# ALiBi attention: row maxima taken per half of the queries, and the order of the first group of heads

## The chip, the cores and the metric

The kernel runs on one core of a Trainium2 chip. The metric is the device time of one execution in microseconds (us). The core has TensorE (PE, matrix products and transposes), VectorE (DVE), ScalarE (ACT, exponentials among others), GpSimd (POOL), and SyncE (SP), which issues DMAs.

## What is computed

Two transformer layers on 1024 tokens of width 512, each an attention and a feed-forward part with a layer norm after each. The change touches the attention of the second layer: 32 heads of width 16, clipped and layer-normed queries and keys, ALiBi bias, causal softmax.

```python
qkv = jnp.clip(jnp.einsum('bsd,ed->bse', hidden_states, w_qkv), -CLIP_QKV, CLIP_QKV)
q, k, v = jnp.split(qkv, 3, axis=-1)
q = _layer_norm(q, q_ln_w, q_ln_b)
k = _layer_norm(k, k_ln_w, k_ln_b)
scores = jnp.einsum('bqhd,bkhd->bhqk', q, k) * scale
scores = jnp.where(causal[None, None], scores + slopes[:, None, None] * rel, -jnp.inf)
probs = jax.nn.softmax(scores, axis=-1)
attn = jnp.einsum('bhqk,bkhd->bqhd', probs, v).reshape(B, S, D)
```

## The kernel before

`program` runs five stages one after the other: `stage_latent` and `stage_mla` (first attention), `stage_front` (first feed-forward part and the projections of q and k of the second layer), `stage_alibi` (the second attention) and `stage_gated` (the rest). The change lies in `stage_alibi` and in two tables ahead of it.

`stage_alibi` works on eight groups of four heads (`GROUPS`, `HG`). For each group it needs queries and keys with the head dimension on the partitions. `build(chunk, which)` transposes queries (0) or keys (1) of two groups on PE (L1367), scales them on DVE (L1503), and ACT and DVE or POOL split them into a high and a low part. `move(eng, g, which, landed)` then copies the pieces of a group with twelve DMAs of 64 KB (L1322) into `qk_bufs`, of which there are three sets (`BUFS`): SP moves queries, POOL moves keys and loads the ALiBi rows. A set holds two blocks of rows of queries (`queries(b, s)`, one for each pair of heads) and four of keys.

The softmax needs the maximum of each score row ahead of the exponentials. `m(g, n)` is one of 24 units (`M_UNITS`): for a pair of heads `s`, the query tile `i` (128 queries, the last tile first) and the key half, PE computes the scores of both heads (L1392, with a mask matmul L1395 on the diagonal) into one of two PSUM slots `sm`, and DVE reduces them to negated maxima (L1515). After the last unit `top` joins the two key halves on DVE and splits the result into two parts (L1525 to L1530), `rows` transposes it on PE (L1401), DVE copies it to `mT` (L1535), and SP's `maxima(g)` writes it with four DMAs (L1334) into two extra rows of the query buffers. From then on a product of keys and queries already holds score minus maximum. `e(g, n)`, 48 a group, is such a product for a key tile, a half of the queries and a head (L1416, mask L1419), into one of three PSUM banks; ACT takes the exponential (L1475). `pv(g, c)` multiplies the four heads' probabilities of a chunk by the values (L1432). `out` copies the result (L1482), `back` transposes it back (L1440) and DVE divides by the row sums.

`alibi_order` writes out one list that PE, ACT and DVE each follow, every engine taking its own kinds. Within group g the 48 e and 12 pv are interleaved with the 24 m of group g+1 (the list `ahead`), its top, the first four m of group g+2, and the rows of group g+1, spread by the number of columns. For group 0 nothing runs ahead: its list begins with the two builds, the value projections `v` of four of the eight token tiles (`project_v`, twelve matmuls each, L78 called from it, into the three banks that e uses later), the 24 m with the other four v between the first ones, top, m(1,0), rows, and three more m of group 1.

SP has its own order: the moves of group 0's queries, a wait for all eight v (`vp`; the buffers that group 1 uses hold operands of v until then), the moves of group 1's queries, `maxima(0)`, and then for each group the moves of group g+2 and `maxima(g+1)`. POOL waits for the same `vp` before it clears and fills the buffers of groups 1 and 2 (`pads`, `load_rows`, `move_keys`), and then clips the values (`values`, L1587) that pv reads.

## Time and profile before

| | us |
|---|---|
| median of 3 runs (lowest to highest) | 1590.12 (1585.02 to 1590.92) |
| the profiled execution | 1588.67 |
| its span, first to last instruction | 1586.8 |
| PE busy | 1477.9 (93%) |
| DVE busy | 893.4 (56%) |
| ACT busy | 805.4 (51%) |
| POOL busy | 549.5 (35%) |
| mean granted clock of TensorE | 0.966 of 2.4 GHz |

The profile is of one execution. Its times are us from the first instruction; names such as L1392 are lines of the kernel. A timeline row gives start, duration, engine, line and operation, output and inputs, and in square brackets how long the engine sat idle before it and what ended that time. The stage that changes runs from about 935 to 1308 us. "e(0,0)" below is the score product at 998.12 us, the first on line L1416.

### The profile page before, as it was taken

To read this page: it belongs to the slowest core of one execution; us is meant where nothing else is said; L and a number is where in the kernel's file an instruction comes from. 1 tells how busy PE (TensorE), PEld (TensorE's weight loads), DVE (VectorE), ACT (ScalarE), POOL (GpSimd) and SP (SyncE) were. 2 spreads that over 40 slices of the span, in tenths; PEclk is the share of its full clock that TensorE was granted. 3 is DMA by queue.
4 is the path that set the end of the run, shared out by engine and by line. 5 is a ranking of instruction groups with operands and counts; after the bars stand their busy time and mean duration, and the time that the engine had idled before them with its cause. 6 is when DMAs were issued, how large, how long until landed. Compare 5 with 4: busy or idle time off the path is not lost. (4 is left out here: it accounts for less than half of the span.)

```text
span 1586.8 us, 23991 instructions
## 1 busy us (share of the span) xinstructions
PE 1477.9 (93%) x8320; PEld 1036.9 (65%) x8320; DVE 893.4 (56%) x1346; ACT 805.4 (51%) x1731; POOL 549.5 (35%) x506
## 2 busy tenths in 40 slices
PE   5499999999999999999968988899999989999996
PEld 4377676667767766776635866555555548888885
DVE  3145454555544555554565745666666616877877
ACT  2266555556655555666423430455555565433343
POOL 0444433344443334444015044223232004444442
PEclk9699999999999999999978997999999999999998
DMA  3135544544454354445530034333333205000000
GB/s 120 49 46 51 50 34 47 42 40 43 48 50 34 46 47 40 39 46 41 84 60 1 1 44 69 48 55 55 55 55 55 88 2 226 1 1 0 1 27 27
DMA packets 46289, 74.06 MB, mean 47 GB/s; under 512 B 18704, under 2 KB 24848, under 8 KB 45328
## 3 DMA queue, kind: packets, MB, share of 16 engines
q1 hardware_dynamic: 41872, 62.70, 28.4%
q0 software_dynamic: 4352, 10.49, 4.4%
q8 instruction: 41, 0.67, 0.2%
q14 instruction: 24, 0.20, 0.0%
HBM read 40.39 MB, written 2.10 MB: 27 GB/s over the span
## 5 line engine op out<-in xcount | busy, mean ns | idle before, releaser
L677 DVE TENSOR_REDUCE nmax<-sc 128x1 f32<-128x128 f32 (+7 forms) x256 | 192.4, 752 | 182.7 <-PE sc L465 182.7
L1515 DVE TENSOR_REDUCE pm<-l_sm 128x2 f32<-128x1024 f32 (+1 forms) x192 | 179.8, 957 | 112.6 <-PE l_sm L1395 61.8
L1475 ACT ACTIVATE l_probs<-l_banks 128x512 f32<-128x512 f32 (+3 forms) x384 | 171.2, 493 | 136.1 <-PE l_banks L1419 97.1
L608 ACT COPY pt<-tb 128x512 f32<-128x512 f32 (+3 forms) x256 | 129.2, 505 | 201.4 <-PE tb L479 199.8
L600 ACT ACTIVATE probs<-sc,nmax 128x128 f32<-128x128 f32 (+7 forms) x256 | 190.6, 745 | 56.2 <-DVE nmax L677 55.9
L479 PE MATMUL tb<-ident,probs 128*128 128x128 f32 x1152 | 174.1, 276 | 2.1 <-ACT pt L608 1.1
L78 PE MATMUL sc<-k_h,q_h 128*128 128x512 f32 (+3 forms) x384 | 144.7, 377 | 22.1 <-POOL q_l L748 14.6
L1416 PE MATMUL l_banks<-qk_bufs 128*128 128x512 f32 (+3 forms) x384 | 141.3, 412 | 5.2 <-ACT l_probs L1475 3.8
L1392 PE MATMUL l_sm<-qk_bufs 128*128 128x512 f32 (+3 forms) x384 | 130.8, 412 | 12.9 <-DVE pm L1515 6.5
L503 PE MATMUL mb<-pt,ckv 128*64 128x512 f32 (+3 forms) x768 | 137.8, 494 | 0.1
L78 PE MATMUL sc<-k_l,q_h 128*128 128x512 f32 (+3 forms) x384 | 133.7, 348 | 0.0
L78 PE MATMUL sc<-k_h,q_l 128*128 128x512 f32 (+3 forms) x384 | 133.6, 348 | 0.0
L479 PEld LDWEIGHTS tb<-ident,probs 128*128 128x128 f32 x1152 | 123.5, 142 | 8.1 <-DVE pt L685 4.0
L668 DVE TENSOR_TENSOR x_tok<-mb,x_tok 128x512 f32<-128x512 f32 x128 | 88.0, 688 | 61.0 <-PE mb L78 59.5
L1416 PEld LDWEIGHTS l_banks<-qk_bufs 128*128 128x128 f32 x384 | 72.1, 193 | 67.5 <-ACT l_probs L1475 42.7
L78 PEld LDWEIGHTS sc<-k_h,q_h 128*128 128x128 f32 x384 | 72.8, 190 | 58.1 <-issue 34.8
L730 POOL TENSOR_TENSOR ol_l<-ol_f,ol_h 128x512 fp32r<-128x512 f32 x32 | 41.3, 1292 | 192.0 <-ACT ol_h L587 191.9
L748 POOL TENSOR_TENSOR q_l<-late,q_h 128x1024 fp32r<-128x1024 f32 x32 | 76.0, 2375 | 51.4 <-ACT q_h L593 51.3
L503 PEld LDWEIGHTS mb<-pt,ckv 128*64 128x64 f32 x768 | 49.7, 136 | 65.5 <-issue 57.3
L1918 POOL TENSOR_TENSOR wall_l<-gated_late,wall_h 128x512 fp32r<-128x512 f32 x44 | 57.1, 1319 | 97.9 <-ACT wall_h L1824 97.9
L1977 DVE RECIPROCAL late<-late 128x512 f32<-128x512 f32 x27 | 90.5, 3352 | 0.8
L1392 PEld LDWEIGHTS l_sm<-qk_bufs 128*128 128x128 f32 x384 | 75.4, 208 | 23.7 <-DVE pm L1515 13.7
(263 smaller groups left out, 3145.2 us busy)
## 6 DMA issues: line engine op xcount, KB each, us to landing
gated_late<-in_gated SPq DMA_DIRECT2D x11, 768.0 KB, 14.0
wout<-in_w_out SPq DMA_DIRECT2D x16, 512.0 KB, 7.1
late<-late SPq DMA_DIRECT2D x128, 64.0 KB, 2.0
rb<-rT SPq DMA_DIRECT2D x64, 128.0 KB, 8.8
qk_bufs<-late SPq DMA_DIRECT2D x96, 64.0 KB, 5.0
qk_bufs<-late POOLq DMA_DIRECT2D x96, 64.0 KB, 5.9
nope_t<-in_nope_by_dim SPq DMA_DIRECT2D x16, 192.0 KB, 5.6
late<-in_gated SPq DMA_DIRECT2D x3, 768.0 KB, 9.1
```

Source lines behind the costliest of these rows:

```text
L78: last = pe.matmul(out, l, r, start=start and n == 0, stop=stop and n == len(terms) - 1)
L479: last = pe.transpose(tb[TB[g]][:, b, :], probs[n % 4][:, (j0 + b) * P:(j0 + b + 1) * P], keep.ident[:])
L503: last = pe.matmul(mb[g][64 * e:64 * e + 64, off:BANK], keep.ckv[:, j, :], pt[g][:, e, j, off:BANK], start=(j == 0), stop=(j == 4 * g + 3))
L600: act.activation(probs[s][:, 0:w], sc[n % 2][:, 0:w], ACT.Exp, bias=nmax[:, s:s + 1], accum_out=ssum[:, n:n + 1]).then_inc(exped, 1)
L608: act.copy(pt[i // 4][:, e, j0:j0 + nb, (i % 4) * P:(i % 4 + 1) * P], tb[TB[g]][:, 0:nb, :]).then_inc(pt_act, 1)
L668: dve.tensor_tensor(keep.x[:, j, :], mb[OUT_BANK[j]][:], keep.x[:, j, :], ALU.add).then_inc(mb_read[OUT_BANK[j]], 1)
L677: dve.tensor_reduce(nmax[:, n % 4:n % 4 + 1], sc[n % 2][:, 0:(n // 2 + 1) * P], AX.X, ALU.max, negate=True).then_inc(negmax, 1)
L1392: last = pe.matmul(dst[:, par, 0:w], queries(b, s)[:, i * P:(i + 1) * P], keys(b, 2 * s + par)[:, c0:c0 + w], start=True, stop=not diagonal)
L1416: last = pe.matmul(banks[:, at, 0:w], keys(b, h)[:, j * P:(j + 1) * P], queries(b, h // 2)[:, q0:q0 + w], start=True, stop=not diagonal)
L1475: act.activation(probs[(NC * g + c) % RING][:, h, 0:w], banks[:, (E_STEPS * g + n) % SLOTS, 0:w], ACT.Exp).then_inc(exped, 1)
L1515: dve.tensor_reduce(pm[g % 2][:, :, s, i, half], slot(("m", g, n))[:, :, 0:w], AX.X, ALU.max, negate=True).then_inc(freed, 1)
L1977: dve.reciprocal(den[:], den[:]).then_inc(rec_ok, 1)
```

## The change

The maxima are kept in two halves of the queries: part 0 for query tiles 0 to 3, part 1 for tiles 4 to 7. `M_UNITS` takes tiles 3, 2, 1, 0 first, then 7, 6, 5, 4. `top`, `rows` and `maxima` exist per part, each on half of the data, so a group has two of each, and `rows_in` has a semaphore per part; e(g, n) waits for part 0 at n = 0 and for part 1 at n = 16, from where its queries are of the second half. The query buffers are laid out so that a half of both pairs is contiguous, which makes each row of a query move two pieces. In the list, six of the eight v stand ahead of the first m, and a v is four items, one for each quarter of the contraction; the last two are placed, quarter by quarter, behind m(0,0) to m(0,7). Group 0's top and rows of part 0 follow, then four more m, then its e(0,0..15) and pv(0,0..2) between m(0,13..23), then part 1. POOL waits for `v_ev` instead of `vp` and clips the values of group 0 ahead of the pads of group 1, those of group 1 behind its key moves.

The diff, without the lines that only pass the new arguments on:

```diff
@@ -1194,14 +1194,17 @@
     k[:, :, 0] = k[:, :, 1] = 1.0
     q[:, :, 2], q[:, :, 3], q[:, :, 4], q[:, :, 5] = sh, sl, -pos, -pos
     k[:, :, 2], k[:, :, 3], k[:, :, 4], k[:, :, 5] = pos, pos, sh, sl
+    q = np.ascontiguousarray(q.reshape(GROUPS, 2, EX, 2, 2, BANK).transpose(0, 1, 2, 4, 3, 5)).reshape(q.shape)
     return q, k
 
 
 CHUNKS = [(j, half) for half in range(2) for j in range(4 * (half + 1))]
 NC = len(CHUNKS)
 E_STEPS = HG * NC
-M_UNITS = [(s, i, half) for i in reversed(range(ST)) for half in range(i // 4 + 1) for s in range(HG // 2)]
+M_UNITS = [(s, i, half) for i in (3, 2, 1, 0, 7, 6, 5, 4) for half in range(i // 4 + 1) for s in range(HG // 2)]
 NM = len(M_UNITS)
+M_HALF = 4 * (HG // 2)
+C_HALF = 4
 AHEAD = 4
 
 
@@ -1220,27 +1223,41 @@
 
 def alibi_order():
 
-    order = [("build", 0, 0), ("build", 0, 1)] + [("v", 0, j) for j in range(4)]
-    for n in range(NM):
-        order.append(("m", 0, n))
-        if n % 2 == 1 and n // 2 < 4:
-            order.append(("v", 0, 4 + n // 2))
-    order += [("top", 0, 0), ("m", 1, 0), ("rows", 0, 0)]
+    order = [("build", 0, 0), ("build", 0, 1)] + [("v", k, j) for j in range(6) for k in range(DK)]
+    late_v = [("v", k, j) for j in (6, 7) for k in range(DK)]
+    for n in range(M_HALF):
+        order += [("m", 0, n), late_v[n]]
+    order += [("top", 0, 0), ("m", 0, M_HALF), ("rows", 0, 0)]
+    order += [("m", 0, n) for n in range(M_HALF + 1, M_HALF + 5)]
+    rest = list(range(M_HALF + 5, NM))
+    at = 0
+    for c in range(C_HALF):
+        for h in range(HG):
+            order.append(("e", 0, HG * c + h))
+            while at < len(rest) and at * C_HALF * HG <= (HG * c + h) * len(rest):
+                order.append(("m", 0, rest[at]))
+                at += 1
+        if c >= 1:
+            order.append(("pv", 0, c - 1))
+    order += [("m", 0, n) for n in rest[at:]]
+    order += [("top", 0, 1), ("m", 1, 0), ("rows", 0, 1)]
     order += [("m", 1, n) for n in range(1, AHEAD)]
     for g in range(GROUPS):
-        ahead = [("m", g + 1, n) for n in range(AHEAD, NM)] if g + 1 < GROUPS else []
+        ahead = []
         if g + 1 < GROUPS:
-            ahead += [("top", g + 1, 0)]
+            ahead += [("m", g + 1, n) for n in range(AHEAD, M_HALF)] + [("top", g + 1, 0), ("m", g + 1, M_HALF), ("rows", g + 1, 0)]
+            ahead += [("m", g + 1, n) for n in range(M_HALF + 1, NM)] + [("top", g + 1, 1)]
         if g + 2 < GROUPS:
-            ahead += [("m", g + 2, 0), ("rows", g + 1, 0)] + [("m", g + 2, n) for n in range(1, AHEAD)]
+            ahead += [("m", g + 2, 0), ("rows", g + 1, 1)] + [("m", g + 2, n) for n in range(1, AHEAD)]
         elif g + 1 < GROUPS:
-            ahead += [("rows", g + 1, 0)]
+            ahead += [("rows", g + 1, 1)]
         if g % 2 == 0 and g // 2 + 1 < GROUPS // 2:
             ahead[2:2] = [("build", g // 2 + 1, 0)]
-            ahead[5:5] = [("build", g // 2 + 1, 1)]
-        done, total = 0, sum(chunk_cols(c)[1] * HG for c in range(NC))
+            ahead[6:6] = [("build", g // 2 + 1, 1)]
+        first = C_HALF if g == 0 else 0
+        done, total = 0, sum(chunk_cols(c)[1] * HG for c in range(first, NC))
         at = 0
-        for c in range(NC):
+        for c in range(first, NC):
             for h in range(HG):
                 order.append(("e", g, HG * c + h))
                 done += chunk_cols(c)[1]
...
         mT = al.sb("mT", [HG * 2 * ST, P], F32R)
         rsum = al.sb("rsum", [P, ST, HG])
         sm = [al.ps(f"l1_sm{i}", [P, 2, BANK]) for i in range(2)]
         banks = al.ps("l1_banks", [P, SLOTS, BANK])
         pv = al.ps("l1_pv", [P, BANK])
...
@@ -1305,7 +1324,12 @@
 
         def queries(b, s):
 
-            return keep.bufs[:, 6 * b + s, :]
+            pair = keep.bufs[:, 6 * b:6 * b + 2, :].rearrange("p a b -> p (a b)")
+            return pair.rearrange("p (half s c) -> p s half c", half=2, s=2)[:, s]
+
+        def query_cols(b, s, c0, w):
+
+            return queries(b, s)[:, c0 // BANK, c0 % BANK:c0 % BANK + w]
 
         def keys(b, h):
 
@@ -1319,26 +1343,28 @@
                 dst, parts = ((queries(b, h // 2), (0, 0, 1)), (keys(b, h), (2, 3, 2)))[which]
                 for n, w in enumerate(parts):
                     r0 = KR * (h % 2) + EX + HD1 * n
-                    eng.dma_start(dst[r0:r0 + HD1, :].bitcast(F32), stages[w][src, :]).then_inc(landed[b], 16)
+                    eng.dma_start(dst[r0:r0 + HD1].bitcast(F32),
+                                  stages[w][src, :] if which else stages[w][src, :].rearrange("p (half c) -> p half c", half=2)).then_inc(landed[b], 16)
 
         with nc.Block() as block:
 
             @block.sync
             def _(sp):
-                def maxima(g):
-                    sp.wait_ge(freed, uses["rows", g, 0] + 1)
+                def maxima(g, part):
+                    sp.wait_ge(freed, uses["rows", g, part] + 1)
                     for par in range(2):
                         for c in range(2):
-                            r, src = KR * par + c, (2 * par + c) * 2 * ST
+                            r, src = KR * par + c, MAXIMA * part + (2 * par + c) * ST
                             b = 6 * (g % BUFS)
-                            sp.dma_start(keep.bufs[r:r + 1, b:b + 2, :].bitcast(F32),
-                                         mT[src:src + 2 * ST, :].bitcast(F32)).then_inc(rows_in, 16)
+                            sp.dma_start(keep.bufs[r:r + 1, b + part, :].bitcast(F32),
+                                         mT[src:src + ST, :].bitcast(F32)).then_inc(rows_in[part], 16)
 
                 sp.wait_ge(low, 1)
                 move(sp, 0, 0, moved)
                 sp.wait_ge(vp, ST)
                 move(sp, 1, 0, moved)
-                maxima(0)
+                maxima(0, 0)
+                maxima(0, 1)
                 for g in range(GROUPS):
                     if g + 2 < GROUPS:
                         if g >= 1:
@@ -1351,7 +1377,8 @@
                             sp.wait_ge(alibi_in[done % BUFS], LOADS * (done // BUFS + 1))
                         prefetch_gated(sp, io, keep)
                     if g + 1 < GROUPS:
-                        maxima(g + 1)
+                        for part in range(2):
+                            maxima(g + 1, part)
 
             @block.tensor
             def _(pe):
...
@@ -1368,13 +1395,16 @@
                                             keep.ident[:])
                     last.then_inc(turned, 1)
 
-                def project_v(j):
-                    from_one(pe, v_ev, j - SLOTS + 1)
-                    rows, terms = slice(j * P, (j + 1) * P), []
-                    for k in range(DK):
-                        terms += [(keep.xT_h[:, k, rows], keep.wv_h[:, k, :]), (keep.xT_l[:, k, rows], keep.wv_h[:, k, :]),
-                                  (keep.xT_h[:, k, rows], keep.wv_l[:, k, :])]
-                    three(pe, banks[:, j % SLOTS, :], terms).then_inc(vp, 1)
+                def project_v(j, k):
+                    if k == 0:
+                        from_one(pe, v_ev, j - SLOTS + 1)
+                    rows = slice(j * P, (j + 1) * P)
+                    last = three(pe, banks[:, j % SLOTS, :], [(keep.xT_h[:, k, rows], keep.wv_h[:, k, :]),
+                                                              (keep.xT_l[:, k, rows], keep.wv_h[:, k, :]),
+                                                              (keep.xT_h[:, k, rows], keep.wv_l[:, k, :])],
+                                 start=k == 0, stop=k == DK - 1)
+                    if k == DK - 1:
+                        last.then_inc(vp, 1)
 
                 def m(g, n):
 
...
                     b, at = g % BUFS, (E_STEPS * g + n) % SLOTS
-                    if n == 0:
-                        pe.wait_ge(rows_in, ROWS * (g + 1))
+                    if n in (0, HG * C_HALF):
+                        pe.wait_ge(rows_in[n // (HG * C_HALF)], ROWS * (g + 1))
                         if g == 0:
                             pe.wait_ge(v_ev, ST)
                     from_one(pe, exped, E_STEPS * g + n + 1 - SLOTS)
...
                                       negate=True).then_inc(freed, 1)
 
-                def top(g):
-
-                    own = uses["m", g, NM - 1] + 1
-                    dve.wait_ge(freed, own)
+                def top(g, part):
+
+                    done = 2 * g + part
+                    dve.wait_ge(freed, uses["m", g, (M_HALF, NM)[part] - 1] + 1)
                     if g >= 1:
-                        dve.wait_ge(rows_ps, g)
-                    part = pm[g % 2]
-                    dve.tensor_copy(nmax[:, :, :, 0:4], part[:, :, :, 0:4, 0]).then_inc(joined, 1)
-                    dve.tensor_tensor(nmax[:, :, :, 4:8], part[:, :, :, 4:8, 0], part[:, :, :, 4:8, 1], ALU.min).then_inc(joined, 1)
-                    dve.wait_ge(joined, 3 * g + 2)
-                    dve.tensor_copy(nmax_hl[:, :, 0].bitcast(F32R), nmax[:]).then_inc(joined, 1)
-                    dve.wait_ge(joined, 3 * g + 3)
-                    dve.tensor_tensor(nmax_hl[:, :, 1], nmax[:], nmax_hl[:, :, 0], ALU.subtract).then_inc(split, 1)
-
-                def rows(g):
-                    from_one(dve, rows_in, ROWS * g)
-                    dve.wait_ge(rows_ps, g + 1)
-                    dve.tensor_copy(mT[:], slot(("rows", g, 0))[0:HG * 2 * ST, 0, 0:P]).then_inc(freed, 1)
+                        dve.wait_ge(rows_ps, done - 1)
+                    got = pm[g % 2]
+                    if part == 0:
+                        dve.tensor_copy(nmax[:, 0], got[:, :, :, 0:4, 0]).then_inc(joined, 1)
+                    else:
+                        dve.tensor_tensor(nmax[:, 1], got[:, :, :, 4:8, 0], got[:, :, :, 4:8, 1], ALU.min).then_inc(joined, 1)
+                    dve.wait_ge(joined, 2 * done + 1)
+                    dve.tensor_copy(nmax_hl[:, part, :, 0].bitcast(F32R), nmax[:, part]).then_inc(joined, 1)
+                    dve.wait_ge(joined, 2 * done + 2)
+                    dve.tensor_tensor(nmax_hl[:, part, :, 1], nmax[:, part], nmax_hl[:, part, :, 0], ALU.subtract).then_inc(split, 1)
+
+                def rows(g, part):
+                    from_one(dve, rows_in[part], ROWS * g)
+                    dve.wait_ge(rows_ps, 2 * g + part + 1)
+                    dve.tensor_copy(mT[MAXIMA * part:MAXIMA * part + MAXIMA, :],
+                                    slot(("rows", g, part))[0:MAXIMA, 0, 0:P]).then_inc(freed, 1)
 
                 def back(g):
                     dve.wait_ge(back_ps, g + 1)
...
@@ -1594,15 +1627,16 @@
                     pool.wait_ge(ones, PADS[0] + 2 * u + 1)
                     pool.memset(vx[u][:, :, :, HD1:HD1 + 1], 1.0).then_inc(ones, 1)
                     pool.wait_ge(ones, PADS[0] + 2 * u + 2)
-                pool.wait_ge(vp, ST)
+                pool.wait_ge(v_ev, ST)
+                values(0, 0)
+                pool.wait_ge(vx_ok, 1)
                 for b in range(1, BUFS):
                     pads(b)
                     load_rows(b)
                     if b == 1:
                         move_keys(1)
-                pool.wait_ge(v_ev, ST)
-                for u in range(2):
-                    values(u, u)
+                        values(1, 1)
+                        pool.wait_ge(vx_ok, 2)
                 for g in range(GROUPS):
                     if 1 <= g and g + 2 < GROUPS:
                         pool.wait_ge(sE, E_STEPS * g)
```

## Rows read from the trace of the kernel before

**Rows 1.** The page: engine totals, and the granted clock in 40 slices.
```profile
PE 1477.9 (93%) x8320; PEld 1036.9 (65%) x8320; DVE 893.4 (56%) x1346; ACT 805.4 (51%) x1731; POOL 549.5 (35%) x506
...
PEclk9699999999999999999978997999999999999998
```

**Rows 2.** Busy time in stretches: PE, PEld, DVE, ACT, POOL, granted clock, DMA, GB/s.
```profile
950.00:956.00 6.00, 0.04 (x1) 0.00 (x0) 0.00 (x0) 0.58 (x1) 0.47 (x2) 0.79 0.76 107
...
960.00:962.00 2.00, 2.00 (x9) 1.44 (x8) 0.00 (x0) 0.03 (x1) 0.00 (x0) 0.93 0.00 0
...
974.00:979.40 5.40, 4.02 (x15) 2.04 (x13) 4.71 (x5) 1.60 (x2) 5.05 (x6) 0.81 0.58 105
...
979.40:992.00 12.60, 11.96 (x42) 7.96 (x42) 9.08 (x13) 0.00 (x0) 12.14 (x20) 0.50 0.98 150
...
998.10:1012.20 14.10, 12.73 (x82) 7.85 (x80) 10.46 (x9) 7.76 (x17) 5.08 (x3) 1.00 0.19 33
...
1037.30:1277.00 239.70, 232.65 (x1638) 132.43 (x1637) 148.00 (x187) 138.61 (x308) 51.87 (x90) 1.00 0.33 60
```

**Rows 3.** Timeline, PE, 938 to 966 us: start, duration, instruction, idle before.
```profile
938.04 12.00 PE L78 MATMUL l_banks<-qk_bufs 128*128 128x512 f32 x48
...
956.04 2.07 PE L1392 MATMUL l_sm<-qk_bufs 128*128 128x512 f32 x4 [6.00 <-DMA qk_bufs<-late]
...
957.91 4.02 PE L78 MATMUL l_banks<-qk_bufs 128*128 128x512 f32 x12
...
961.77 0.39 PE L1392 MATMUL l_sm<-qk_bufs 128*128 128x512 f32 x1
...
963.11 3.00 PE L78 MATMUL l_banks<-qk_bufs 128*128 128x512 f32 x12
```

**Rows 4.** Groups by form on DVE, 974 to 992 us: busy, mean ns, idle.
```profile
L1515 DVE TENSOR_REDUCE pm<-l_sm 128x2 f32<-128x1024 f32 x6 | 7.2, 1223 | 3.4 <-PE l_sm L1392 2.3 <-PE l_sm L1395 0.9
```

**Rows 5.** Lines L1322 (moves) and L1334 (maxima): issue ns, times, us to landing.
```profile
L1322 SPq DMA_DIRECT2D qk_bufs<-late x12: 554/642/1677, 940.9 to 951.6; - x12
...
L1322 SPq DMA_DIRECT2D qk_bufs<-late x12: 507/589/597, 973.7 to 980.6; - x12
...
DMA to landing us min/median/max: 2.2/5.5/7.8
...
L1334 SPq DMA_DIRECT2D qk_bufs<-mT x4: 520/582/591, 994.4 to 996.2; - x4
...
DMA to landing us min/median/max: 1.8/1.8/1.8
```

**Rows 6.** Timeline, 991 to 999 us: the chain to the first exponential score.
```profile
991.53 0.60 DVE L1525 COPY nmax<-pm 128x16 f32<-128x16 f32 x1
...
994.11 0.27 DVE L1535 CAST mT<-l_sm 64x128 fp32r<-64x128 f32 x1
...
998.12 0.50 PE L1416 MATMUL l_banks<-qk_bufs 128*128 128x512 f32 x1
```

**Rows 7.** Timeline, PE and DVE, around the starts of groups 1 and 7.
```profile
1030.88 1.06 PE L1432 MATMUL l_pv<-l_probs,vx 128*32 128x512 f32 x8
...
1032.91 0.28 DVE L1535 CAST mT<-l_sm 64x128 fp32r<-64x128 f32 x1 [0.70 <-PE l_sm L1401]
...
1039.74 0.50 PE L1416 MATMUL l_banks<-qk_bufs 128*128 128x512 f32 x1
...
1273.64 0.30 PE L1416 MATMUL l_banks<-qk_bufs 128*128 128x128 f32 x1
...
1273.82 0.31 PE L1416 MATMUL l_banks<-qk_bufs 128*128 128x128 f32 x1
...
1276.52 0.50 PE L1416 MATMUL l_banks<-qk_bufs 128*128 128x512 f32 x1 [1.35 <-DMA qk_bufs<-mT]
...
1276.90 0.47 PE L1416 MATMUL l_banks<-qk_bufs 128*128 128x512 f32 x1
...
1277.25 0.47 PE L1416 MATMUL l_banks<-qk_bufs 128*128 128x512 f32 x1
```

More of the change, by code:

```diff
@@ L1415, in e @@
                     diagonal = q0 == j * P
-                    last = pe.matmul(banks[:, at, 0:w], keys(b, h)[:, j * P:(j + 1) * P], queries(b, h // 2)[:, q0:q0 + w],
+                    last = pe.matmul(banks[:, at, 0:w], keys(b, h)[:, j * P:(j + 1) * P], query_cols(b, h // 2, q0, w),
                                      start=True, stop=not diagonal)
@@ L1486, in _ @@
                         build(g, n)
-                    elif kind == "v":
+                    elif kind == "v" and g == DK - 1:
                         v_out(n)
```

26 lines of the change are left out of this document (14 added, 12 removed).

## The prediction

> **What bounds the kernel now.** I read the page's engine totals first: TensorE (PE) is busy 93% of the span, and after the start its granted clock sinks in slices 21 and 22, in the stage before, and in slice 25, 952 to 992 us, the front of the ALiBi stage, where the change lies [rows 1]. Next come the stretches of the stage one by one [rows 2]. From 1037.3 to 1277 us PE is busy 232.65 of 239.7 us at full clock, while VectorE (DVE) is busy 148 us and ScalarE (ACT) 139 us: PE is the bound there, and only PE work taken away would pay. Before 998 us it is different. From 950 to 956 PE did 0.04 us of work; from 974 on DVE's maxima set the pace; and from 979.4 to 992 the granted clock is 0.50, that is 1.2 instead of 2.4 GHz. So the third view is the timeline of 934 to 998 us. PE projects v(0..3) in 12.00 us, 0.25 us a matmul, then idles 6.00 us until the moves of group 0's queries and keys have landed at 956.04 [rows 3]. The maxima m(0, 0..23) follow with the other four v between them, and after 991.53 the chain that every group needs: the minima joined (`top`), a transpose (`rows`), the copy to mT at 994.11, four DMAs into the query rows, and the first exponential score e(0,0) at 998.12 [rows 6].
>
> How much is lost before 998.1? PE work from 934.7 on, at full clock: two builds 3.3 us, 96 matmuls of v at 0.25 = 24, 24 units of m 11.6 (a unit of 512 columns with its masks 0.67 us: two between 961.77 and 963.11 [rows 3]; by columns I take 0.56, 0.45 and 0.33 for the diagonal 384, 256 and 128, and 0.45 for 512 without mask), m(1,0..3) 2.3 and a transpose 0.3: 41.5 of 63.4 us. 22 us are lost to waits and to the lower clock; that is what the change can draw on.
>
> **The change part by part.** All times are on the profiled run's own clock.
>
> *v in quarters, six of them ahead.* 72 matmuls at 0.25 us fill 938.04 to 956.1. The 6.00 us of idle time go, as does the lowered clock behind it: the mean of 950 to 956 is 0.79, and the v projection that follows m(0,1) in the list takes 4.02 us where the next takes 3.00 [rows 3]. What is late next is the same landing, 956.04. It is reached by twelve SP issues, the last started at 951.6 [rows 5]. The new query layout writes each 4 KB row as two pieces. No row shows such a move. Bounds: 0 (the same bytes) and the last move's tail doubled, 4.4 us more. The tail is mostly queueing of bytes that do not change, so I take 0.5: m(0,0) at 956.5.
>
> *m(0,0..7) with the last eight quarters.* PE: 2 x (0.67 + 0.56 + 0.45 + 0.33) = 4.0, plus 8 x 0.75 = 6.0. DVE needs at most 1.22 us a unit [rows 4] against 1.42 for PE's pair, so PE sets it: 966.5.
>
> *The wait that replaces it: SP's queue.* `maxima(0,0)` stands behind `wait_ge(vp, ST)` and `move(sp, 1, 0)`. vp is now complete at 966.5, and the twelve issues need what they needed from 973.7 on, 6.9 to the last start and 0.59 for it, 7.5 us [rows 5]: 974.0. mT is ready long before: top at 966.9, and the old chain from top to mT took 2.9 us [rows 6], so 969.8. The four DMAs, now half as large, cost their number: 3.7 us from the first issue (0.3 after 994.11, the copy's end) to e at 998.12, with 1.8 to land [rows 5, 6]. They now run beside POOL's key moves of group 1; between 0 and 6 us (the longest that group's moves took to land was 7.8 [rows 5], against 1.8) I take 0.5, since SP's own queue is empty by then. e(0,0) starts at 978.2. Meanwhile PE has only m(0,8..12), five units that DVE paces to about 973; PE is idle from 971.5 to 978.2. The clock will be at 1.2 GHz by then, as it came down in 950 to 956 and by 979.4 [rows 2].
>
> The Trainium skill speaks against this split: "DMA: Bandwidth & Descriptors", section "Anatomy of one DMA", gives a DMA a fixed cost of about 2 us, whatever its size. The trace agrees, with 1.8 us for these transfers. By that rule halving them buys no landing time, and doubling their number only adds issues; the sum is the same by either, because each later set of four finds SP's queue idle.
>
> *e(0,0..15), pv(0,0..2) and m(0,13..23).* e costs 0.35 us at 512 columns and 0.18 at 128 (1276.90 to 1277.25, 1273.64 to 1273.82 [rows 7]); with 0.29 and 0.24 between, 4 x 1.06 = 4.2. The three pv: about 1.0 for 512 columns [rows 7], and 0.75 and 0.55 by columns, 2.3. The eleven m: 5 x 0.45 + 2 x (0.56 + 0.45 + 0.33) = 4.9. Together 11.4 at full clock; DVE needs 5 x 1.22 and some 4.1 by columns for the rest, 10.2, so PE bounds it, if barely. I add 10% for waits as in 998.1 to 1012.2 (12.73 busy of 14.1 [rows 2]) and 2 us for about 4 us at the lower clock, the time it took to come back from 956.04 (0.93 in 960 to 962 [rows 2]): 14.6, to 992.8.
>
> *The chain again, top(0,1) to e(0,16).* As from 991.53 to 998.12, 6.6 us [rows 6]: 999.4. Nothing hides it but m(1,0..3), as before.
>
> *The sum of the front.* Before, e(0,0) starts at 998.1; after, e(0,16) starts at 999.4, with 4.2 + 2.3 = 6.5 us of PE work already behind it. Gain 6.5 - 1.3 = 5.2. Against it: the remaining 24 m, two builds and both tops of group 1 must now fit beside 32 instead of 48 exponentials: DVE 27 of some 35 us, where group 0 used to have 41 (998.1 to 1039.7 [rows 6, 7]). Between 0 and 3 I take 1.0. For a clock that sinks again in the chain, between 0 and 2, I take 0.5. Left: 3.7.
>
> *Steady state, seven groups.* Each gains one PE transpose, three small DVE operations (two more of top's, a second mT copy), and four SP issues on a queue idle most of the time. PE bounds here, so the transpose counts, some 0.27 (a 128-column product's record is 0.30 [rows 7]); DVE's additions hide under PE (148 of 239.7 busy) unless a full score slot lets them through. Between 0 and 1.3 a group (the spacing of a whole m reduce) I take 0.27 x 6 = 1.6 after group 1. Returned: e(7,0) waited 1.35 us for the last mT [rows 7]; its rows are ready half a group earlier, and e(7,16) has 16 exponentials for cover. Balance -0.3. The units of m in another order, the pool's `values(0,0)` ahead of its pads (0.6 us by the 0.60 of a small copy [rows 6]; POOL's work for group 1 now starts behind v near 967, where it started behind v near 974, as SP's moves did [rows 5], and m(1,0) comes at 992), and the strided query views: nothing, since each is covered by 6 us or more; if that cover is gone, the POOL part costs its 0.6.
>
> *The end.* 3.7 - 0.3 = 3.4 us off 1588.67, the profiled run: 1585.3. That run is 1.45 below the median of the three shown; splitting that, **1586**.
>
> **The rivals.** (1) *The front goes better.* The q layout costs nothing, PE's clock is back at once in the e phase, and the second chain at full clock takes 5.5: 956.1, 966.1, 977.3, + 12.5 = 989.8, 995.3. Gain 6.5 + 2.8 = 9.3, with no loss in group 1, steady +0.3: 1579. For it: the e phase opens with full-width matmuls. Against: PE did five short units in the 12 us before.
>
> (2) *Slower: the lower clock holds through the e phase.* From 979.4 to 992 the clock stayed at 0.50 although PE was busy 11.96 of 12.6 us, with the same kind of units, and it was back only by 998.1 [rows 2]. Then 11.4 us become 22.8: 978.2 to 1001.0, the chain to 1007.6, 9.5 late against 6.5 of work moved, +3.0; 2 us more for e(0,16) on at the lower clock, 1 in group 1, 0.3: 1588.67 + 6.3 = 1595. It decides the sign once e(0,16) starts later than 998.1 + 6.5 = 1004.6. Against it: full-width matmuls without mask and pv stand in the phase, and the clock did return after 956 to such a mix.
> The Trainium skill ("TensorE: Matmul & The Clock Gate", "HAM oscillation — how this bites in real kernels") says that waits on DMA between bursts bring the lower clock back each time; the 0.79 of 950 to 956 agrees, and by it the wait on SP's queue here has its price in either case.
>
> (3) *The steady state pays.* The second top and rows cost PE a slot wait of 1 us in each of seven groups (PE waits where it must run m right after a transpose whose copy queues behind a reduce). Front as forecast, +7: 1592. For it: DVE sat 0.70 us idle before a mT copy [rows 7]. Against: with one set, 232.65 of 239.7 us were busy.
>
> (4) *The change does not reach its aim:* e(0,16) starts so late that no work is gained, 1588 to 1590; part of the forecast's range.
>
> **How the numbers follow.** Forecast (with 4) 0.50, rival 1 0.23, rival 2 0.14, rival 3 0.13. About 0.5%, 8 us, is what a measurement of this kernel tells from no change; against the median of 1590.12 faster means under 1582.2 and slower over 1598. Under 1582.2 lie rival 1 and a little of the forecast, 0.26; over 1598 only the far end of rivals 2 and 3, 0.06; the rest 0.68. The range takes in 1579 and 1595 and little beyond, with some noise of the runs: 1577 to 1595.
>
> **What would show it.** PE busy without a gap from 938 to 966. A PE gap that ends near 978, released by the DMA from mT; SP's first L1334-type issue right behind twelve moves. e(0,16) near 999, and the granted clock near 0.5 from about 972 to 982. e(1,0) near 1036 (before 1039.7). The pace of the later groups unchanged, 39.5 us each (1039.74 to 1276.52 for six [rows 7]). The prediction is wrong if e(0,0) starts before 975 (SP's queue no obstacle), if the q moves land after 958, if the clock is low throughout the e phase, or if a later group changes by over 0.5 us.

## The result, and the profile after

The median went from 1590.12 us to 1597.79 us (1596.52 to 1598.17), a ratio of 1.006 with a 95% interval of 1.0036 to 1.0083: slower by 7.7 us, where 3.4 us of gain and at worst 1595 were forecast. The profiled execution took 1596.52 us against 1588.67.

From the page of the kernel after, the engine totals and the clock in 40 slices, which answer to [rows 1]:

```profile
PE 1479.6 (93%) x8328; PEld 1036.8 (65%) x8328; DVE 903.4 (57%) x1370; ACT 807.6 (51%) x1731; POOL 550.2 (34%) x506
...
PEclk9699999999999999999979997899999999999998
```

PE does 1.7 us more work, so most of the loss is idle time. The stage ahead of the change ended 2.5 us earlier in this profiled run (the first v product starts at 935.53, before at 938.04). So I compare from that product on, here and for all kernels: "+44.8" is 44.8 us after its own first v product. That product starts between 931.4 and 937.6 in the profiled runs of the changed kernels, and before's 938.04 is the latest. The code ahead of it is the same, and the traces show where the spread comes from: the clock stood at 0.50 for 66.5 us ahead of that product in before, 63.1 in after and 49.7 in the run whose product starts at 931.4 (e11), and over all thirteen traces the start follows this time (correlation 0.97). Before's run is among those with most of it. So for all kernels but e5 what the differences behind this product add up to, up to e(7,0), lies 1 to 4 us above what the medians show.

| us after the first v product | before | forecast | after |
|---|---|---|---|
| m(0,0) | 18.0 | 18.5 | 18.1 |
| last m ahead of `top(0,0)` and last v done | - | 28.5 | 28.1 |
| first DMA of `maxima(0,0)` issued | - | 36.0 | 36.9 |
| e(0,0) | 60.1 | 40.2 | 44.8 |
| e(0,16) | - | 61.4 | 66.8 |
| e(1,0) | 101.7 | 98.0 | 108.1 |
| from e(1,0) to e(7,0) | 236.8 | 237.0 | 240.9 |

Against before: 6.4 us lost until e(1,0), 4.2 in the six groups behind it, less the 2.5 of the stage ahead and 0.2 in what follows: 7.9, the 7.85 us between the two profiled runs.

The timeline of PE after, 953 to 1014 us (start, duration, instruction, idle before and what ended it):

```profile
953.60 0.50 PE L1422 MATMUL l_sm<-qk_bufs 128*128 128x512 f32 x1 [0.67 <-DMA qk_bufs<-late]
...
968.72 1.22 PE L1422 MATMUL l_sm<-qk_bufs 128*128 128x512 f32 x2
980.33 0.79 PE L1446 MATMUL l_banks<-qk_bufs 128*128 128x512 f32 x1 [10.39 <-DMA qk_bufs<-mT]
...
1002.34 0.80 PE L1446 MATMUL l_banks<-qk_bufs 128*128 128x512 f32 x1 [1.43 <-DMA qk_bufs<-mT]
...
1013.87 0.28 PE L1431 MATMUL l_sm<-ident,nmax_hl 128*32 128x128 f32 x1 [1.60 <-DVE late L1533]
```

The 6.00 us of idle time before m(0,0) are 0.67 now. In their place PE waits 10.39 us for the DMAs from mT, until 980.33, which is e(0,0). Busy time in stretches, with the columns of [rows 2] (PE, PEld, DVE, ACT, POOL, granted clock, DMA, GB/s):

```profile
954.00:960.00 6.00, 6.00 (x34) 4.23 (x34) 4.63 (x5) 0.59 (x1) 0.00 (x0) 1.00 0.00 0
...
972.00:978.00 6.00, 0.00 (x0) 0.00 (x0) 0.00 (x0) 0.00 (x0) 5.86 (x13) 0.50 1.18 169
...
984.00:992.00 8.00, 8.00 (x55) 4.67 (x54) 6.06 (x7) 3.96 (x10) 0.00 (x0) 0.93 0.36 33
...
1002.00:1004.00 2.00, 1.66 (x6) 1.22 (x6) 0.03 (x1) 0.60 (x1) 0.00 (x0) 0.54 0.00 0
1004.00:1008.00 4.00, 4.00 (x19) 3.47 (x18) 2.13 (x3) 0.60 (x1) 0.00 (x0) 0.50 0.02 4
...
1012.00:1014.00 2.00, 0.40 (x4) 0.14 (x2) 1.93 (x5) 0.25 (x2) 0.10 (x1) 1.00 0.19 30
```

From 972 to 978 PE does nothing at all, while POOL issues its loads and key moves (969 to 977) and the transfer engines move 169 GB/s. The clock is at 1.0 behind the v products, falls at 968.0, 2 us ahead of that wait, stays at 0.50 through it, and is back to 0.93 in 984 to 992: most of the exponential phase does not run at the lower clock. It falls again at 1002.2, with the second wait for mT, and 1004 to 1008 run at 1.2 GHz. Why e(0,0) comes so late is seen on SP, the engine that issues these DMAs. Lines L1346 (moves, 931 to 1000 us) and L1359 (maxima, 960 to 980 us), in the form of [rows 5]:

```profile
L1346 SPq DMA_DIRECT2D qk_bufs<-late x24: 585/597/2203, 938.4 to 971.8; - x24
```
```profile
L1359 SPq DMA_DIRECT2D qk_bufs<-mT x4: 634/660/769, 972.5 to 974.7; - x4
```

mT was ready by 965.7, but the first small DMA starts at 972.5, right behind the last of the twelve moves at 971.8. And from that first issue to e(0,0) it takes 7.9 us (980.33 - 972.46), where before it took 3.7 [rows 5, 6].

The third place is on DVE and POOL, in the first group with builds. Timeline of DVE and of POOL:

```profile
1009.86 2.27 DVE L1556 COPY nmax<-pm 128x16 f32<-128x16 f32 x1
1012.17 0.17 DVE L1560 CAST nmax_hl<-nmax 128x16 fp32r<-128x16 f32 x1
...
1012.47 1.34 DVE L1533 TENSOR_SCALAR late<-l_sm,qk_ln 128x1024 f32<-128x1024 f32 x1
```
```profile
1009.73 2.38 POOL L1611 TENSOR_TENSOR late<-late 128x1024 fp32r<-128x1024 f32 x1 [26.06 <-ACT late L1493]
```

A copy of 16 elements a partition takes 2.27 us instead of 0.17, and it ends when POOL's subtraction ends. Behind it come the cast, the remainder (both 0.17) and the scaling of a build (L1533, 1.34 us). PE waits 1.60 us until that scaling has ended and it can transpose the rows, in the stretch of 1012 to 1014 in which it is busy 0.40 of 2 us.

### The profile page after: what moved, and what is told of

It is laid out like the page before. It is cut to its first block and busy times, and to the rows that moved or that the text cites. A ratio compares the mean times of both kernels' runs of the same rounds, so it can differ in the third digit from the quotient of the medians.

```text
span 1594.7 us, 24093 instructions
## 1 busy us (share of the span) xinstructions
PE 1479.6 (93%) x8328; PEld 1036.8 (65%) x8328; DVE 903.4 (57%) x1370; ACT 807.6 (51%) x1731; POOL 550.2 (34%) x506
## 5 line engine op out<-in xcount | busy, mean ns | idle before, releaser
L1505 ACT ACTIVATE l_probs<-l_banks 128x512 f32<-128x512 f32 (+3 forms) x384 | 172.8, 493 | 151.5 <-PE l_banks L1449 93.2
L1446 PE MATMUL l_banks<-qk_bufs 128*128 128x512 f32 (+3 forms) x384 | 145.5, 419 | 14.4 <-DMA qk_bufs<-mT 11.8
L78 PEld LDWEIGHTS sc<-k_h,q_h 128*128 128x128 f32 x384 | 72.8, 190 | 58.1 <-issue 35.1
L503 PEld LDWEIGHTS mb<-pt,ckv 128*64 128x64 f32 x768 | 49.7, 136 | 65.6 <-issue 57.3
```

Of the source, the lines that this page charges most:

```text
L78: last = pe.matmul(out, l, r, start=start and n == 0, stop=stop and n == len(terms) - 1)
L503: last = pe.matmul(mb[g][64 * e:64 * e + 64, off:BANK], keep.ckv[:, j, :], pt[g][:, e, j, off:BANK], start=(j == 0), stop=(j == 4 * g + 3))
L1446: last = pe.matmul(banks[:, at, 0:w], keys(b, h)[:, j * P:(j + 1) * P], query_cols(b, h // 2, q0, w), start=True, stop=not diagonal)
L1505: act.activation(probs[(NC * g + c) % RING][:, h, 0:w], banks[:, (E_STEPS * g + n) % SLOTS, 0:w], ACT.Exp).then_inc(exped, 1)
```

## The experiments

Each kernel was timed in five rounds beside the kernel before on the same chip. Before's median is 1588.29 us beside e1 to e4, 1588.43 beside e5 to e8 and 1587.65 beside e9 to e11. Ratios are to before in the same set, with the 95% interval. "Below after" compares medians of separate sets; since before stood at 1590.12 us beside after, such a gain is 1.7 to 2.5 us smaller when each kernel is held against its own before. Marks such as +95.1 are from the one profiled run of a kernel. Every kernel computes the whole reference; in two of them PE does filler products beside it.

### Parts of the change alone

**e1_v_ahead**: the kernel before, with only the value projections in quarters, six ahead of m(0,0) and the last two behind m(0,0) to m(0,7).

```diff
-    order = [("build", 0, 0), ("build", 0, 1)] + [("v", 0, j) for j in range(4)]
+    order = [("build", 0, 0), ("build", 0, 1)] + [("v", k, j) for j in range(6) for k in range(DK)]
+    late_v = [("v", k, j) for j in (6, 7) for k in range(DK)]
     for n in range(NM):
-        order.append(("m", 0, n))
-        if n % 2 == 1 and n // 2 < 4:
-            order.append(("v", 0, 4 + n // 2))
+        order += [("m", 0, n)] + late_v[n:n + 1]
```

> The kernel before with one part of the change: v in quarters, six of the eight ahead of the first m, the last two behind m(0,0) to m(0,7). Maxima, queries, SP's and POOL's order as before. Theory A (the 6.00 us of PE idle at the start are on the path): m(0,23) ends some 9 us earlier, m(1,0) then waits for group 1's key moves, which start 7 us earlier, so the first e comes 6 to 7 us earlier: about 1583 to 1584 us. Rival B (the time is only moved into the wait for group 1's keys or for DVE's pace): 1588 to 1590.

Measured: 1580.65 us, 0.9953 [0.9935, 0.9971]. e(1,0) at +95.1 against +101.7. This part alone gains 7.6 us, more than the forecast gave to the whole front. The windows of e1 show what it leaves:

```profile
962.00:975.00 13.00, 11.25 (x45) 7.01 (x44) 10.34 (x13) 1.87 (x2) 10.32 (x16) 0.75 0.73 101
975.00:988.00 13.00, 11.35 (x37) 6.95 (x37) 9.83 (x15) 0.00 (x0) 7.85 (x11) 0.50 0.67 106
```

In the second stretch of the maxima the clock is down to 0.50, PE is busy 11.35 of 13 us and DVE 9.83; which of the two sets the pace there is the question of e7 below.

**e4_unit_order**: the kernel before, with only the order of the units changed (tiles 3, 2, 1, 0, 7, 6, 5, 4).

> The kernel before with the new order of the units of m alone (query tiles 3, 2, 1, 0, 7, 6, 5, 4). Theory A (the later groups pay for the second top and rows): 1590, groups of 39.5 us as before. Rival B (they pay for the unit order, which puts other products beside each other on PE): 40.2 to 40.4 us a group, about 1595.

Measured: 1590.66 us, 1.0021 [1.0009, 1.0032]: 2.4 us slower. The six groups from e(1,0) to e(7,0) take 240.15 instead of 236.8, and group 0 takes 1.6 us more. The same 80 us, two groups of before and of e4, as windows (before, then e4):

```profile
1039.74:1120.37 80.63, 78.20 (x550) 44.66 (x547) 51.43 (x64) 46.64 (x102) 21.42 (x37) 1.00 0.36 54
```
```profile
1039.29:1121.51 82.22, 78.89 (x551) 45.31 (x547) 51.25 (x64) 46.54 (x102) 21.49 (x37) 1.00 0.35 53
```

The same matmuls, give or take a missing record, are 0.7 us longer, and 0.9 us more is idle: PE's waits for ACT's exponentials grow from 1.0 to 1.4 us and those for DVE's maxima from 1.3 to 1.7. What makes these waits longer was not tested. Where the 0.7 arises is seen unit by unit. Timeline of PE, before, then e4, at a narrow unit of m:

```profile
1064.72 0.47 PE L1416 MATMUL l_banks<-qk_bufs 128*128 128x512 f32 x1
1065.03 0.27 PE L1392 MATMUL l_sm<-qk_bufs 128*128 128x128 f32 x1
1065.14 0.23 PE L1395 MATMUL l_sm<-mask,ident_b 128*128 128x128 bf16 x1
```
```profile
1041.33 0.23 PE L1419 MATMUL l_banks<-mask_t,ident_b 128*128 128x128 bf16 x1
1041.36 0.31 PE L1392 MATMUL l_sm<-qk_bufs 128*128 128x128 f32 x1
1041.51 0.23 PE L1395 MATMUL l_sm<-mask,ident_b 128*128 128x128 bf16 x1
```

In before the narrow units come late in a group, between exponential scores without mask; such a product holds PE for 0.11 us (1065.03 to 1065.14). In the new order they come first and stand behind a mask: 0.15 us (1041.36 to 1041.51). For 256 columns it is 0.12 against 0.21 (1063.59 to 1063.71 in before, 1039.67 to 1039.88 in e4). Counted over the two groups, the 48 products of m with 384 columns or fewer hold PE for 9.62 us in e4 against 8.92 in before, and 10 of them against 16 stand right behind a 512-column score product. The reading that the weights of a narrow product load under the wide product ahead of it, and not under a short mask, fits these rows; it was not tested by itself.

**e3_halves_only**: the kernel after, but with group 0 in the old order (v as in before, 24 m, both tops, both rows, no early exponentials).

> The changed kernel with the front of its list as before: four v ahead, four behind the first m, all 24 m, then both tops and both rows, and no e of group 0 ahead of that. It keeps the new unit order, the two tops, rows and sets of small DMAs per group, the query layout and POOL's new order. Theory A (the later groups pay for the halves or the unit order, 0.9 us each in the traces): first e near 999 as before, then 6 to 7 us lost by the end, about 1596. Rival B (the loss of the changed kernel is all in its front): 1590 to 1591.

Measured: 1594.86 us, 1.0041 [1.0026, 1.0056]: 6.6 us slower. The six groups take 240.97 (+4.2), the front is 4.5 us later, of which e4 has 1.6. So the two halves, with the query layout and POOL's order that e3 also keeps, cost most of what the change lost, without any early exponential. In the six groups about 3.4 of the 4.2 go with the unit order (e4), and 0.8 is left for the second top and rows, half of the 1.6 of the forecast.

### What delays the first exponentials

**e2_sp_first**: the kernel after, with the small DMAs of part 0 ahead of the moves of group 1 on SP.

```diff
                 move(sp, 0, 0, moved)
+                maxima(0, 0)
                 sp.wait_ge(vp, ST)
                 move(sp, 1, 0, moved)
-                maxima(0, 0)
                 maxima(0, 1)
```

> The changed kernel with maxima(0,0) issued by SP ahead of the wait for v and of the twelve moves of group 1's queries. Theory A (in the changed kernel e(0,0) is late by SP's queue, where the four small DMAs stand behind twelve moves): first issue near 966 instead of 972.5, landing in about 4 us since nothing else is in flight, e(0,0) near 970 instead of 980.3, 8 to 10 us less than the changed kernel, 1588 to 1590. Rival B (the landing is slow by the load of POOL's key moves and the clock stays low all the same): 2 us or less gained, 1596.

Measured: 1587.38 us, 1.0000 [0.9988, 1.0013]: 10.4 us below after. e(0,0) comes at +34.9 instead of +44.8. The issues start at 967.7, and e(0,0) starts at 971.95 with no idle time before it. Of the 9.9 us, 6.2 are the queue (first issue at +30.7 instead of +36.9) and 3.6 the landing (4.2 us from first issue to e(0,0) instead of 7.9): POOL's loads for group 1 start only at 971.2 here. What PE then waits for:

```profile
PE l_sm L1422 <- DMA qk_bufs<-late: 3.3, 1, 3.3
PE l_sm L1431 <- DVE late L1533: 1.4, 1, 1.4
...
PE l_banks L1446 <- DMA qk_bufs<-mT: 0.3, 1, 0.3
```

(The waits of PE in e2, 960 to 1015 us: total, times, longest. The last row is the one before e(0,16).) The 10 us of idle time before e(0,0) are gone, and 7.6 of the 9.9 are left at e(0,16) (+59.2). What is late next are the keys of group 1, 3.3 us at one m(1,n), and the rows behind a build, 1.4. The copy of `top(1,0)` is not the one held up here; it began just ahead of POOL's subtraction, and the cast behind it was held up instead:

```profile
1003.28 0.17 DVE L1556 COPY nmax<-pm 128x16 f32<-128x16 f32 x1
1003.49 2.24 DVE L1560 CAST nmax_hl<-nmax 128x16 fp32r<-128x16 f32 x1
```
```profile
1003.30 2.39 POOL L1611 TENSOR_TENSOR late<-late 128x1024 fp32r<-128x1024 f32 x1 [17.60 <-ACT late L1493]
```

**e6_pool_held**: the kernel after, with POOL's loads and key moves of group 1 held back until the small DMAs of part 0 have landed.

```diff
                     pads(b)
+                    if b == 1:
+                        pool.wait_ge(rows_in[0], ROWS)
                     load_rows(b)
```

> The changed kernel with POOL holding back its loads and key moves of group 1 until the four small DMAs of part 0 have landed. Theory A (these took 7.8 us from the first issue to the landing, against 3.7 before, because POOL's 64 KB moves share the DMA engines): e(0,0) 4 us earlier, near 976.3 on the changed kernel's clock, 4 us less in all unless m(1,0) then waits for its keys: 1594. Rival B (they wait behind SP's own twelve moves of group 1's queries): e(0,0) at 980 as before, no gain.

Measured: 1590.76 us, 1.0015 [1.0006, 1.0024], 7.0 us below after. In e6 L1359 and PE read:

```profile
L1359 SPq DMA_DIRECT2D qk_bufs<-mT x4: 634/660/769, 974.4 to 976.7; - x4
```
```profile
978.47 0.80 PE L1446 MATMUL l_banks<-qk_bufs 128*128 128x512 f32 x1 [6.01 <-DMA qk_bufs<-mT]
```

From the first issue (974.42) to e(0,0) it is 4.05 us, against 7.87 in after with the same four issues, and the issues still cost 0.63 to 0.77 us each. So the 3.8 us are the landing, and POOL's traffic makes it: four loads of 128 KB and twelve moves of 64 KB beside four small transfers. SP's own twelve moves stand ahead of the small DMAs in both kernels. The gain grows behind it, from 3.7 us at e(0,0) to 5.9 at e(1,0); the next section says why.

### What is lost behind e(0,16)

**e5_builds_later**: the kernel after, with the builds of the next pair placed behind the rows of part 0 in the list (index 8 and 12 instead of 2 and 6).

> The changed kernel with the two builds of the next pair of groups placed behind rows(g+1, 0) in the list instead of before and between top and rows. Theory A (in the even groups the join of part 0, a DVE copy, stands 2.3 us beside POOL's subtraction, and in group 0 PE waits 1.6 us for rows behind the build's scaling on DVE): the copy back at 0.17 us in all groups, that wait gone, 3 to 5 us less than the changed kernel, 1593 to 1595. Rival B (DVE has room there, the cost lies elsewhere): 1597 to 1598.

Measured: 1591.53 us, 1.0023 [1.0013, 1.0034], 6.3 us below after. The copy of `top`, in after and in e5 (ns min/median/max):

```profile
L1556 DVE COPY nmax<-pm x8: 174/176/2398, 963.5 to 1253.3; 128x16 f32<-128x16 f32 x8
```
```profile
L1556 DVE COPY nmax<-pm x8: 174/175/176, 961.6 to 1242.7; 128x16 f32<-128x16 f32 x8
```

No copy is long any more, and no cast. In the six groups e5 gains 2.1 us on after, in the two of them that hold a build. From e(0,16) to e(1,0) it takes 35.1 us, after 41.3. That stretch in after, e6, e9 (below) and e5:

```profile
1002.34:1043.64 41.30, 37.69 (x211) 21.00 (x211) 28.15 (x34) 18.00 (x35) 10.72 (x15) 0.88 0.23 40
```
```profile
1000.60:1039.53 38.93, 34.63 (x211) 19.43 (x211) 28.11 (x34) 18.00 (x35) 10.72 (x15) 0.96 0.25 42
```
```profile
996.44:1034.78 38.34, 36.44 (x210) 21.08 (x210) 26.97 (x35) 18.19 (x35) 10.72 (x15) 0.88 0.23 43
```
```profile
1000.14:1035.21 35.07, 32.66 (x210) 18.60 (x210) 26.16 (x34) 17.99 (x35) 10.72 (x15) 1.00 0.25 47
```

The last columns are the granted clock, the DMA share and GB/s. The clock differs as well as the order, and the pairs of equal order tell the two apart. The early builds are in after and e6: 10.1 and 3.4 us at the lower clock, 41.3 and 38.9 us in all. The late ones are in e9 and e5: 9.4 and 0 us, 38.3 and 35.1. Both pairs give 0.35 us lost for each us at 0.50. My estimate from this is that some 3.5 of the 6.2 us between after and e5 are the clock, and 2.7 the place of the builds. The profiled run of e5 is also the fastest of its seven (1585.84 us, median 1591.53); with each held against its own before, e5 gains 4.6 us on after, which is near 2.7 and 2.1 together with nothing for the clock.

**e9_both_mended**: the kernel after with e2's and e5's edit.

> The changed kernel with both mends: SP issues maxima(0,0) first, as in e2, and the builds stand behind rows(g+1, 0), as in e5. Theory A (two separate losses, in the front and in group 0, add up; what is left of the cost is the unit order and the second top and rows in the later groups): e(1,0) 95.5 to 96.5 us after the first v (before 101.7, e2 98.4, e5 102.1), six groups 239.2 us, about 1584 to 1585. Rival B (both mends relieve the same wait): 1587, as e2.

Measured: 1583.00 us, 0.9971 [0.9960, 0.9982]. Both mends together turn 7.7 us of loss into 4.7 of gain. The front did not reach what was expected, though: e(1,0) at +99.0 beside e2's +98.4. The trace shows what took it. Up to e(0,16) both kernels have the same order, but the keys of group 1 came later here, and PE waited 4.80 us for them instead of 3.30:

```profile
988.96 0.79 PE L1422 MATMUL l_sm<-qk_bufs 128*128 128x512 f32 x1 [4.80 <-DMA qk_bufs<-late]
```

Behind e(0,16) the clock then stayed at 0.50 for 9.4 us, in e2 for 3.9. In the six groups e5's part shows in full, 238.8 instead of 241.0.

### Are the early exponentials worth it?

**e8_first_group**: e2, but with halves only in group 0; the later groups take their units in the old order, with both tops and both rows at the end.

> The kernel of e2_sp_first with the halves put to use in group 0 alone: groups 1 to 7 take their units in the old order, with both tops and both rows at the end. Theory A (six groups pay 3.4 us for the unit order and 1 to 1.5 for the second top and rows; early exponentials in group 0 gain less than v ahead alone): 3 to 4 us less than e2, about 1583 to 1584, still above e1's 1581. Rival B (the early exponentials are worth more once the later groups do not pay for them): below 1580.

Measured: 1580.88 us, 0.9956 [0.9944, 0.9968]; six groups 237.5, front +96.7. Relieved of the unit order in later groups, the change gains what e1 gains (1580.65) and nothing more: e(0,0) is 17.8 us earlier than in e1, and e(1,0) 1.6 later. In between PE waits 3.3 us for group 1's keys, as in e2. Whether early exponentials pay once these keys are moved first, as e10 below does for e1, was not tested.

**e11_unit_mix**: e1 with the tiles in the order 7, 6, 3, 2, 1, 0, 5, 4.

> The kernel of e1_v_ahead with the query tiles of m in the order 7, 6, 3, 2, 1, 0, 5, 4. Theory A (the unit order costs in e4 because its narrow masked products no longer stand behind the unmasked 512-column products of e, under which their weights load): this order puts most narrow units there, groups as short as e1's 39.5 us or up to 0.5 us shorter: 1578 to 1581. Rival B (the cost comes with any unit order other than the old one, from waits on DVE and ACT): 1583 to 1585.

Measured: 1579.13 us, 0.9953 [0.9938, 0.9968], six groups 236.6: not every order costs. Of the 48 products of 384 columns or fewer in two groups, 16 stand right behind a 512-column score, as in before (e4: 10), and the pace is before's. That fits the reading of e4 and does not single it out, since PE's idle time is back at before's too.

### The lower clock in the maxima

**e7_v_ahead_filler**: e1, and in the later maxima of group 0 PE does one or two 512-column products more after each unit, into the bank of pv, read by nobody.

```diff
                         m(g, n)
+                        if (g == 0 and n >= 8) or (g == 1 and n < AHEAD):
+                            filler(2 if m_cols(n)[1] == BANK else 1)
```

> The kernel of e1_v_ahead with filler: behind m(0,8) to m(0,23) and m(1,0) to m(1,3) one or two further products of 512 columns (40 units, 30-odd products) into the bank that pv uses later, read by nobody. It only adds PE work where DVE sets the pace. Theory A (the 1.2 GHz of that stretch costs time: at that clock PE, busy 11.35 of 13 us, paces the units, not DVE): the clock stays at 2.4, the maxima end 3 us earlier, the first exponentials run at full speed: 3 to 5 us less than e1, 1576 to 1578. Rival B (DVE bounds the stretch at either clock): same as e1 or 1 to 2 us more, 1581 to 1583.

Measured: 1579.59 us, 0.9942 [0.9929, 0.9954]. Windows of e7, and what then ends PE's idle time:

```profile
962.00:975.00 13.00, 12.57 (x65) 8.28 (x63) 11.59 (x14) 1.87 (x2) 12.28 (x19) 1.00 0.89 126
975.00:988.00 13.00, 10.57 (x40) 6.82 (x41) 7.44 (x13) 0.21 (x1) 5.80 (x8) 0.74 0.56 80
```
```profile
979.47 1.19 PE L1394 MATMUL l_sm<-qk_bufs 128*128 128x512 f32 x2 [2.18 <-issue]
```

The clock stays at 1.0 until 979.4, and the maxima of group 0 end 2.0 us earlier, at +43.5 instead of +45.5. So the lower clock did cost time there, and DVE alone had not set the pace. (The 40 units of the expectation are 20 in the kernel, with 30 products.) But then PE waits 2.18 us at m(1,0). The profile names nothing that ends this wait; in e10 the same product waits for the keys' DMA. The clock falls at its end, and e(1,0) is where it was (+95.14, e1 +95.10). By the medians e7 is 1.1 us below e1, in separate sets with intervals that overlap.

**e10_keys_first**: e7, with POOL's loads and key moves of group 1 ahead of its pads.

> The kernel of e7_v_ahead_filler with POOL issuing the loads and key moves of group 1 before it clears the buffers of groups 1 and 2, instead of behind 3.66 us of clearing. Theory A (the filler ended the maxima 2 us earlier, but m(1,0) then waited 2.2 us for group 1's keys): the wait goes, first e 2 us earlier, 1577 to 1578. Rival B (the chain of mT and the small DMAs, now in a full DMA queue, takes it back): 1579 to 1580 as e7.

Measured: 1578.20 us, 0.9944 [0.9927, 0.9962]; e(1,0) at +93.2. m(1,0) still waits 1.52 us for the keys, and e(0,0) now 1.18 for mT, but the clock is at 1.00 in every window up to 990. The trace shows 1.9 us gained on e7's front, while the intervals of the two overlap. Its median is the lowest of all, 9.4 us below before; its interval overlaps those of e1, e7, e8 and e11.

## Why the prediction was wrong

**Right: the idle time at the start.** PE is busy without a gap to 953 and m(0,0) waits 0.67 us. The new query layout, costed at 0.5 us between 0 and 4.4, costs nothing (+18.07, before +18.00). The eight units with v between them end where they were put. e1 shows that this alone was worth 7.6 us. The prediction gave it no price of its own; to the whole front it gave 3.7.

**Right: what replaces it.** SP's queue was named as the wait, and the first small DMA does stand right behind the twelve moves, 0.9 us later than put. e2 takes it away and gives back 10.4 us. That is more than the forecast's own price for the queue, 4.2 us (first issue at 974.0, mT ready at 969.8): in the trace the queue was 6.2 of e2's 9.9 us, and 3.6 were the landing, which is no longer beside POOL's traffic.

**Wrong term: the landing.** Between 0 and 6 I took 0.5 for the four DMAs beside POOL's key moves, "since SP's own queue is empty by then". It was 4.2 (7.87 against 3.7), and e6 shows that the other queue was the cause: its transfers, and not SP's, were what to price the landing by. With the queue's 0.9 this puts e(0,0) 4.6 us late of the forecast.

**About right: the exponential phase and the second chain.** 15.3 us against 14.6, and 6.7 against 6.6. The clock came back as forecast. Rival 2, the clock low through the phase, did not occur; e(0,16), 66.8 us after the first v, lies level with its turning point (1004.6, or 66.6 from the same start), where the front was to come out even. It came out 6.4 us behind.

**Wrong step: "now fit beside 32 instead of 48 exponentials", 1.0 us between 0 and 3, and 0.5 for the clock.** From e(0,16) to e(1,0) it took 41.3 us, not 36.6. Without these two terms the forecast has 35.1 us for this stretch, and e5, with the builds later and the clock at 1.00, takes 35.07: the rest of the sum fits here. So 6.2 us stand against the 1.5 put, by the estimate above 2.7 instead of 1.0 for DVE and 3.5 instead of 0.5 for the clock. The prediction counted DVE's work and not what stands next to what in the list. The second build, moved by one place only, stands between `top(1,0)` and its rows, and so between a copy and the rows that PE waits for; there POOL's subtraction blocks the copy (in e2 and e6 the cast), and the build's scaling stands ahead of the rows. As for the clock, it fell twice in this stretch of after, at 1002.2 for 6.8 us and at 1015.8 for 3.4.

**Wrong step: "The units of m in another order ... nothing, since each is covered by 6 us or more".** In the later groups the cover was the wrong thing to look at: PE is the bound there, so each matmul's own length and each short wait count, and both changed with the order. e4 prices it at 3.4 us over six groups, against 0 put; in the two groups measured 0.7 of 1.6 us are longer matmuls. The second top and rows, 1.6 us in the sum, measured 0.8 (e3 less e4). Rival 3 put the loss into these groups and was wrong in mechanism: they lost 4.2 us, and the larger part of it comes without a second top and rows. In time rival 2 (1595) was the nearest to the measured 1597.79, and it did not occur either; that it is near is chance.

**The sum.** Relative to the first v: forecast -3.7 at e(1,0), measured +6.4. Of the 10.1 between, 4.6 arise up to e(0,0), 0.8 in phase and second chain, 4.7 behind e(0,16). The later groups add 3.9 (forecast +0.3, measured +4.2), and the earlier end of the stage ahead in the profiled run takes 2.5 off. The would-show list stood right up to the issue of the small DMAs and failed from the landing on: e(0,0) was 2 us past the 978 named, although this run's first v product was 2.5 us early.

**Open.** Why the time at the lower clock ahead of the changed stage differs from run to run of the same code; how exactly e5's 6.3 us divide, for the shares above are an estimate; why the keys of group 1 land 1.5 us later in e9 than in e2; what lengthens PE's waits for ACT and DVE under e4's order, which is half of its cost; and whether the narrow products lengthen by their weight loads.

## What to carry to other kernels

Before a result is asked for earlier, look at the queue of whoever delivers it, and at the other queues that transfer in that moment: here four small DMAs stood behind twelve large ones and landed beside twelve more, and one moved line gave back 9 to 10 us. When items are spliced into a list by index, read the list that comes out: an index moved by one put a build between a maximum and its use. And where the bound engine is full, the order of its instructions has a price of its own; run each part of a change alone, for here one part held all the gain (1580.65 us), the early exponentials added nothing to it as they were tried, and the halves with their order of units only cost.

## What the runs showed of the hardware

- A DVE copy of 128x16 fp32 values took 2.27 us instead of 0.17 beside a POOL subtraction of 2.38 us that had begun 0.13 us earlier, and ended with it. [rows 6] holds a small case of it, 0.60 us beside POOL's value clipping, which the prediction read only as the price of a small copy. It is not the copy alone: in e2 and e6, where the copy had begun 0.02 us ahead of POOL and took 0.17, the cast of 128x16 behind it took 2.24 and 2.23 us. The Trainium skill, "SBUF — State Buffer", section "Who interferes with whom", has the rule: the port pair that DVE and POOL share is an exclusive lock, held for a whole instruction. By that rule the copy waits for POOL's whole instruction, however small the copy is; the traces agree.
- Four small DMAs took 4.05 us from first issue to use with POOL's queue held back and 7.87 with it at work. Each of the four SP issues took 0.63 to 0.77 us in both, so POOL's traffic is not what lengthens them from the 0.52 to 0.59 of before.
- A score product of 128 columns held PE for 0.11 us behind a 512-column product and 0.15 behind a 128-column mask, one of 256 columns 0.12 and 0.21 (before and e4).
- In e1 PE was busy 5.28 of the 6.5 us before the granted clock went to 0.50 at 968.5, with short waits for DVE between, and it stayed there for 24 us although PE was then busy 11.35 of 13 us by the records. With filler products between (e7, 6.35 busy of the same 6.5 us) it stayed at 1.00, and fell at the end of the 2.18 us of waiting that followed.
- The same wait need not have the same end. At e(7,0) PE waited 1.35 us for mT in before and 1.42 in e1. In before the clock stayed at 1.00; in e1 it went to 0.50 for 6.9 us, and the 48 score products of the last group took 30.0 us instead of 27.5.
